# Last two output projections taken row tile by row tile behind the accumulators' turn, and the feed forward weights split on GpSimd

## What is computed

```
x  = layer_norm(x) * g1 + b1;  h = layer_norm(x @ W + b) * g2 + b2
n  = layernorm(h)
for each of 16 heads: q, k, v = n @ W_Q, n @ W_K, n @ W_V
                      p = softmax(causal(q @ k.T / sqrt(128)));  z = p @ v
h  = h + sum over heads of z @ W_O
n  = layernorm(h);  scale = max(max(|n|) / 448, 1e-7)
h  = h + fp8(n / scale) @ (weight * weight_scale) + bias
```

## Time and profile before

| what | value |
|---|---|
| median of 3 runs | 274.49 us (274.19 to 275.79) |
| the profiled execution | 274.52 us, span 272.7 us |
| TensorE busy | 97% of the span |
| VectorE / ScalarE busy | 57% / 47% |
| GpSimd busy | 0.2 us, 4 instructions |
| granted TensorE clock | full speed in all 40 slices |
| HBM read | 22.79 MB |

### The profile page before, as it was taken

The page is one execution under the profiler, slowest core; times in us unless marked ns, Lnnn a source line. Parts: engine busy times, 40 slices in busy tenths (PEclk is TensorE's granted clock), DMA queues, the critical chain, the costliest instruction groups (busy, mean ns, idle before and its releaser), DMA issues.

```text
span 272.7 us, 3956 instructions
## 1 busy us (share of the span) xinstructions
PE 264.4 (97%) x1506; PEld 225.6 (83%) x1506; DVE 156.6 (57%) x325; ACT 129.5 (47%) x220; POOL 0.2 (0%) x4
## 2 busy tenths in 40 slices
PE   6899999999999999999999999999999999999995
PEld 6434446999999999999999999999999999988963
DVE  4579878555545536264555445363555454578892
ACT  2664952364535443544435344445545354356460
POOL 0000000000000000000000000000000000000000
PEclk9999999999999999999999999999999999999999
DMA  6999000124314040413223040404133100000004
GB/s 169 335 288 394 6 0 1 54 102 154 101 55 154 0 154 0 154 19 135 58 96 132 22 154 0 154 0 154 19 135 95 59 0 0 0 4 0 0 2 135
DMA packets 5444, 23.82 MB, mean 87 GB/s; under 512 B 1019, under 2 KB 1483, under 8 KB 3260
## 3 DMA queue, kind: packets, MB, share of 16 engines
q1 hardware_dynamic: 5436, 23.71, 25.9%
HBM read 22.79 MB, written 0.92 MB: 87 GB/s over the span
## 4 chain that ended last, share of the span: by engine, by line
PE 92%; DVE 3%; DMA 2%; SPq 1%; ACT 1%; issue 1%; DVEq 0%
PE bank L274 15%; PE bank L275 15%; PE bank L276 15%; PE acc L309 10%; PE acc L411 8%; PE bank L387 5%; PE bank L395 5%; PE acc L415 4%; PE bank L401 2%; PE acc L524 2%; PE bank L380 2%; DMA tokw_raw<-tok_w 2%; PE bank L282 2%; PE acc L479 1%; PE acc L494 1%; SPq L228 1%
## 5 line engine op out<-in xcount | busy, mean ns | idle before, releaser
L274 PE MATMUL bank<-ht_hi,qkvw_hi 128*128 128x448 f32 (+2 forms) x204 | 74.7, 366 | 0.5 <-DVE ht_lo L749 0.5
L275 PE MATMUL bank<-ht_lo,qkvw_hi 128*128 128x448 f32 (+2 forms) x204 | 73.3, 359 | 0.0
L276 PE MATMUL bank<-ht_hi,qkvw_lo 128*128 128x448 f32 (+2 forms) x204 | 73.2, 359 | 0.0
L749 DVE TENSOR_TENSOR qkvw_lo<-raw,qkvw_hi 128x1536 fp32r<-128x1536 f32 x16 | 28.1, 1758 | 30.7 <-ACT qkvw_hi L546 30.7
L274 PEld LDWEIGHTS bank<-ht_hi,qkvw_hi 128*128 128x128 f32 x204 | 38.4, 188 | 3.7 <-issue 0.6
L276 PEld LDWEIGHTS bank<-ht_hi,qkvw_lo 128*128 128x128 f32 x204 | 38.3, 188 | 3.3
L275 PEld LDWEIGHTS bank<-ht_lo,qkvw_hi 128*128 128x128 f32 x204 | 38.4, 188 | 3.0
L749 DVE TENSOR_TENSOR z_lo<-bank,z_hi 128x448 fp32r<-128x448 f32 x15 | 9.4, 624 | 43.2 <-ACT z_hi L546 43.2
L309 PE MATMUL acc<-tokw_raw,xt 128*112 128x512 f32 x64 | 29.3, 598 | 0.9 <-DMA tokw_raw<-tok_w 0.9
L546 ACT CAST qkvw_hi<-raw 128x1536 fp32r<-128x1536 f32 x16 | 23.6, 1482 | 0.0
L309 PEld LDWEIGHTS acc<-tokw_raw,xt 128*112 128x112 f32 x64 | 10.6, 176 | 14.1 <-issue 9.6
(11 more groups left out here) (122 smaller groups left out, 355.8 us busy)
## 6 DMA issues: line engine op xcount, KB each, us to landing
raw<-heads_w SPq DMA_DIRECT2D x16, 1024.0 KB, 4.9
tokw_raw<-tok_w SPq DMA_DIRECT2D x4, 512.0 KB, 6.9
x_in<-patches SPq DMA_DIRECT2D x3, 448.0 KB, 8.7
ffnw_raw<-ffn_w SPq DMA_DIRECT2D x1, 1024.0 KB, 18.5
out<-h_sb SPq DMA_DIRECT2D x3, 224.0 KB, 2.3
x_in<-patches SPq DMA_DIRECT2D x2, 224.0 KB, 3.0
g_row<-tok_g SPq DMA_DIRECT2D x1, 224.0 KB, 11.2
b_row<-tok_b SPq DMA_DIRECT2D x1, 224.0 KB, 11.6
```

Source lines behind the costliest of these rows:

```text
L274: nc.tensor.matmul(ps, hi, whi, start=first, stop=False, skip_group_check=True)
L275: nc.tensor.matmul(ps, hi, wlo, start=False, stop=False, skip_group_check=True)
L276: return nc.tensor.matmul(ps, lo, whi, start=False, stop=last, skip_group_check=True)
L749: return nc.vector.tensor_tensor(dst, src, hi.bitcast(F32), ALU.subtract)
```

## The change

The turn of the accumulators moves on TensorE from ahead of the transposes of head 14's probabilities to behind the transposes of head 15's values. Behind it head 14's and head 15's output projections go by row tile: tile 0 and tile 1 of head 14 around `weigh_values`, tile 0 and 1 of head 15, and then each of tiles 2 and 3 with both heads in turn. `o_ps` is counted once less, so VectorE's waits for it drop by one. On ScalarE the last exponential stands ahead of the copy of v. The scaling, the cast and the subtraction of the feed forward weights leave VectorE and ScalarE and become a GpSimd block of their own, which waits only for its data (`ffnw_landed`, `late_landed`). VectorE waits for `late_landed` ahead of its part of the heads instead of behind the turn.

```diff
@@ tensor
             project(1, bank[1], s, k_ps)
-            pe.wait_ge(turned_ok, KD)
-            for t in range(TILES):
-                for c in range(KD):
-                    residual_turn(t, c)
             prob_transposes(h - 1)
...
             weigh_values(h - 1)
             value_transposes(h)
 
-            pe.wait_ge(outw_hi_ok, h)
-            pe.wait_ge(outw_lo_ok, h)
-            pe.wait_ge(z_hi_ok, h)
-            for z, w, after in ((z_hi, outw_hi, prob_transposes), (z_hi, outw_lo, weigh_values),
-                                (z_lo, outw_hi, None)):
-                if z is z_lo:
-                    pe.wait_ge(z_lo_ok, h)
-                for t in range(TILES):
-                    last = nc.tensor.matmul(acc[t][0:TR, :], z[:, t, :], w[1 - s][:], start=False, stop=False,
-                                            skip_group_check=True)
-                if after is prob_transposes:
-                    after(h)
-                elif after is weigh_values:
-                    after(h, 0)
-            last.then_inc(o_ps, 1)
...
+            pe.wait_ge(turned_ok, KD)
             for t in range(TILES):
...
+                for c in range(KD):
+                    residual_turn(t, c)
+
+            def project_rows(t, i, z_hi, z_lo):
+                pe.wait_ge(z_hi_ok, HEADS - 1 + i)
+                for z, w in ((z_hi, outw_hi), (z_hi, outw_lo), (z_lo, outw_hi)):
+                    if z is z_lo:
+                        pe.wait_ge(z_lo_ok, HEADS - 1 + i)
+                    last = nc.tensor.matmul(acc[t][0:TR, :], z[:, t, :], w[i][:], start=False,
+                                            stop=(i == 1 and z is z_lo), skip_group_check=True)
+                if i == 1:
+                    last.then_inc(o_ps, 1)
+
+            pe.wait_ge(outw_hi_ok, HEADS)
+            pe.wait_ge(outw_lo_ok, HEADS)
+            prob_transposes(h)
+            project_rows(0, 0, z_hi, z_lo)
+            weigh_values(h, 0)
+            project_rows(1, 0, z_hi, z_lo)
+            project_rows(0, 1, z_last_hi, z_last_lo)
+            project_rows(1, 1, z_last_hi, z_last_lo)
+            for t in range(2, TILES):
+                project_rows(t, 0, z_hi, z_lo)
+                project_rows(t, 1, z_last_hi, z_last_lo)
@@ scalar
             copy_probs(h - 1)
-            act.wait_ge(ffnw_scaled, 1)
-            hi_part(flat_ffnw(ffnw_hi), flat_ffnw(ffnw_raw)).then_inc(ffnw_hi_ok, 1)
+            exponentiate(h)
             copy_v(h)
-            exponentiate(h)
@@ gpsimd
+        @block.gpsimd
+        def _(pool):
+            pool.wait_ge(ffnw_landed, 16)
+            pool.wait_ge(late_landed, 48)
+            nc.gpsimd.tensor_scalar(flat_ffnw(ffnw_raw), flat_ffnw(ffnw_raw), ffn_scale_col[:], None,
+                                    ALU.mult).then_inc(ffnw_scaled, 1)
+            pool.wait_ge(ffnw_scaled, 1)
+            nc.gpsimd.tensor_copy(flat_ffnw(ffnw_hi), flat_ffnw(ffnw_raw)).then_inc(ffnw_hi_ok, 1)
+            pool.wait_ge(ffnw_hi_ok, 1)
+            nc.gpsimd.tensor_tensor(flat_ffnw(ffnw_lo), flat_ffnw(ffnw_raw), flat_ffnw(ffnw_hi).bitcast(F32),
+                                    ALU.subtract).then_inc(ffnw_lo_ok, 1)
@@ vector
+            dve.wait_ge(late_landed, 48)
...
-            dve.wait_ge(ffnw_landed, 16)
-            dve.wait_ge(late_landed, 48)
-            nc.vector.tensor_scalar(flat_ffnw(ffnw_raw), flat_ffnw(ffnw_raw), ffn_scale_col[:], None,
-                                    ALU.mult).then_inc(ffnw_scaled, 1)
...
-            dve.wait_ge(ffnw_hi_ok, 1)
-            lo_part(flat_ffnw(ffnw_lo), flat_ffnw(ffnw_raw), flat_ffnw(ffnw_hi)).then_inc(ffnw_lo_ok, 1)
...
-                dve.wait_ge(o_ps, HEADS + t + 1)
+                dve.wait_ge(o_ps, HEADS + t)
```

More of the change, by code:

```diff
@@ L485, in _ @@
-            last.then_inc(o_ps, 1)
-            pe.wait_ge(outw_hi_ok, h + 1)
-            pe.wait_ge(outw_lo_ok, h + 1)
-            pe.wait_ge(z_hi_ok, h + 1)
-            for t in range(TILES):
[L491 to L496, removed]
+            pe.wait_ge(turned_ok, KD)
```

## The result

The changed kernel takes 281.98 us (median of 4 runs, 280.85 to 282.46) against 274.71 us of the kernel before on the same chip (4 runs, 274.19 to 275.79): a ratio of 1.0242, 95% interval 1.0208 to 1.0275. It is slower by 2.4%. The prediction was 279.2 us in a range of 274.5 to 283.0, and slower by over 1% was its likeliest case. The two profiled executions took 282.25 and 274.52 us, 7.73 apart; the medians are 7.27 apart.

The account below looks back on a forecast made before the run. TensorE, busy for 97% of the span, was taken as the bound, so only its waits count. GpSimd's hold on VectorE (+4.2 us) and the last head (+0.5) on 274.52 gave 279.2 us, range 274.5 to 283.0.

Parts of the forecast that it names:

- likeliest case: Embedding stage: GpSimd at 5.5 to 9 us holds VectorE for whole instructions; 279.2 us, range 277.6 to 281.5, chance 0.42.
- Start and place of GpSimd's work: Middle of the embedding stage: GpSimd starts at 28.8 us, when `ffnw_raw` has landed, where VectorE's chain has little room.
- The mechanism: Embedding stage: VectorE instructions with two SBUF operands wait for the whole rest of GpSimd's instruction; part one +4.2 us.
- The length of GpSimd's work: Three GpSimd instructions over 2048 columns: 2.28 us each, 6.8 in all, between bounds of 5.5 and 19.
- Longer GpSimd: Rival, embedding stage: each microsecond of GpSimd beyond 6.8 shifts TensorE by one; 281 to 283 us, chance 0.15.
- my walk: Embedding stage: two L808 and `nmr` wait for GpSimd in turn, `nmr` 5.9 us late, first projection 4.2 late.
- The last head: Part two, new order on TensorE: padding starts later by 0.5 us, between -0.2 and +0.9.
- The standing still at v: Last head: TensorE waits some 0.7 us for the copy of v, since the exponential stands ahead on ScalarE.
- Other side: Rival, last head: transposes of v do not stand still, padding starts 0.2 us earlier; 274.3 us, chance 0.10.
- the fixed padding then holds the product back: Behind the last head: padding starts 0.5 us later, so L501 starts at 255.6 and `max_diag`'s gain goes unused.

Follow-up runs that it names:

- pool_memset: Kernel before, its three weight instructions left in place, plus four GpSimd memsets that write SBUF and read nothing; 275.02 us against 275.28, ratio 0.9998.
- pool_in_heads: Changed kernel, each GpSimd instruction also waiting for VectorE's subtraction of one head's weights (sixth, seventh, eighth); 275.57 us against 275.22, ratio 1.0027.
- pool_only: Kernel before with only the three feed forward weight instructions moved to GpSimd, last head as before; 282.51 us against 275.28, ratio 1.0252.
- tail_only: Changed kernel with the three weight instructions back on VectorE and ScalarE, only the last head's new order kept; 275.83 us against 275.28, ratio 1.002.
- pool_pieces: Changed kernel with each GpSimd instruction cut into four of 512 columns at the same early place; 276.20 us against 275.22, ratio 1.0043.

## Why the prediction was right, and where it was off

**Start and place of GpSimd's work: right.** 28.8 us was forecast, 28.85 is when the wait ended, and the first instruction starts at 29.28.

**The mechanism: right.** VectorE's instructions with two operands in SBUF are held by a GpSimd instruction that reads SBUF; `pool_memset` takes away the reading and with it the loss, `pool_in_heads` takes away the meeting. With the rule of the Trainium skill quoted in the forecast (SBUF — State Buffer, "Who interferes with whom") this trace agrees in direction both ways; its "whole instruction" agrees with L734 (42.82 and 42.83) and not with L729, which let VectorE go 1.65 us before its recorded end.

**The length of GpSimd's work: the mis-sized term.** I took 2.28 us for each instruction, 6.8 in all; undisturbed they take 5.44, 1.89 and 4.57, 11.9 in all, and in the changed kernel they last from 29.28 to 42.82. The subtraction, 4.57 us undisturbed, agrees with the 4.5 us of the Trainium skill (GPSIMD Engine Reference, "3.1 Elementwise — side-by-side cycle accounting"). The scaling, which I had put near VectorE's rate, took 5.44; no row had prepared me for that.

**The time: in the range, in part by luck.** The likeliest case put 279.2 us, 4.7 more than before; measured are 7.3 more. The time is that of the rival "Longer GpSimd" (281 to 283 us, chance 0.15), but its rule is not what came: at one microsecond of TensorE for each beyond 6.8, these 11.9 us would have given 279.2 + 5.1 = 284.3, above the range. Two errors went against each other, the length too small and the path too direct; the second is the next point.

**Where it bites: partly wrong.** In my walk each of the three instructions caught the first tile's chain, and `nmr` came last. In truth VectorE went on while GpSimd was still in its first instruction; `nmr` of that tile came at 34.28, 4.4 late, 1.3 of it this execution's later start; TensorE took the tile at 35.53 instead of 34.31, 1.2 late, no more than by that start, so the first hold was hidden from it. The start itself did not add to the loss: in `pool_only` the tiles came within 0.1 us of the kernel before (30.45 for the passes of L309 that stand at 30.37 there), and its first projection was no earlier. The third instruction caught the next tile's chain at L791 and made that 6.9 us late (42.83 against 35.89, which is L784's end in the trace of before). From the end of L791 to the first projection it was 45.06 - 35.89 = 9.17 us before and is 52.37 - 42.83 = 9.54 now, so the 7.3 us are 6.9 of hold and 0.4 behind it. I forecast 4.2. The tile that the end of the hold met was the second and not the first, so 7.0 us of later end (42.82 against the walk's 35.8) became only 3.1 of later first projection (52.37 against 49.3).

**The clock: not in the sum.** The forecast had TensorE standing still for microseconds and did not ask what its clock would do behind that. By the distances above it cost 0.7 us (9.55 against 8.83 with the gap padded); that is worked out across two executions, and the timed runs are too coarse to confirm it.

**The last head: right, with its parts.** Forecast +0.5 at the padding, measured +0.49 here, +0.47 and +0.49 in `tail_only` and `pool_in_heads`. The standing still at v was forecast at 0.7 us and is 0.6 (from the end of the weighing's issue, 246.49 + 0.87, to 247.94), and the copy order is its cause: put back, the wait goes and the padding starts 0.14 us earlier than in the kernel before, as the rival "Other side" had it. `max_diag` gained 0.26 us (from 209.99 behind the first projection to 209.73), forecast was 0.2 at most. Also as forecast, the fixed padding then holds the product back, by 0.79.

## What to carry to other kernels

Before moving work to an idle engine, ask when it starts there, not only where it is needed: here "as soon as its data has landed" put it into the one stretch where VectorE's chain had no room. GpSimd is idle but does not stand apart from VectorE; if its instructions read SBUF, give them the stretches in which VectorE's instructions have at most one operand there (`pool_in_heads`), or cut them into short ones (`pool_pieces`). And where a fixed number of padding passes stands in front of a wait, every reordering ahead of it has to be followed by counting the padding again, or a gain of the chain beside it is thrown away.

## What the runs showed of the hardware

- An instruction of VectorE with one value in each partition and two operands in SBUF takes 3.95 us instead of 0.16 beside a GpSimd instruction that reads SBUF; beside memsets on GpSimd over 7.4 us it takes its usual time.
- The hold is mutual: GpSimd's subtraction took 5.88 us instead of 4.57 when VectorE had come first, and a scaling over 512 columns 2.54 instead of 1.57.
- On GpSimd, over 2048 float32 columns: a product with a value for each partition 5.44 us, a cast 1.89, a subtraction 4.57, a memset 1.80; on VectorE the first and the third took 1.28 and 2.28, on ScalarE the cast 1.91.
- The first of these holds VectorE for 3.8 of its 5.4 us over 2048 columns, and for no more than 0.64 of 1.57 over 512 (L795 in `pool_pieces`). Why it lets go before its end is open.
- After TensorE had stood still for 4.4 us the granted clock was 0.75 over the next 6 us; with padding in the gap it stayed at full speed.
